# Attention with a routed mixture of experts on one core: the prefix product of the routing two steps later, the last four tiles of expert outputs transposed one step earlier

## The chip, the cores and the metric

The kernel runs on one core of a Trainium2 chip. The metric is the device time of one execution in microseconds (us). The core has five engines that run their own instruction lists and meet at semaphores: TensorE (PE in the rows; PEld is its loading of weights, which runs beside its products), VectorE (DVE), ScalarE (ACT), GpSimd (POOL), and SyncE (SP), which here only issues DMAs. Each engine takes its list in order, so an instruction that waits holds up all that stand behind it.

## The reference

2048 rows of 128 numbers are normalised, and two branches are added to the input: attention of all rows over all rows, and a feed-forward part in which each row goes to the two best of eight experts.

```python
xn = layernorm(x)                                   # x: (1, 2048, 128)
q, k, v = split(xn @ w_qkv.T, 3)                    # one head of width 128
attn = softmax(q @ k.T * scale) @ v @ w_proj.T + b_proj
t = xn @ W_in + b_in
probs = softmax(t @ W_gate + b_gate)                # 8 experts
topv, topi = top_k(probs, 2); topv /= sum(topv)
mid = relu(t @ W1[e] + b1[e]); eout = mid @ W2[e] + b2[e]   # 128 -> 512 -> 128
moe = sum over the two chosen e of topv * eout
out = x + attn + (moe @ W_out + b_out)
```

## The kernel before

**Attention.** The queries go in eight groups g = 0 to 7 of 256. Each group takes eight steps k = 0 to 7, and a step is two key tiles of 128: `scores(i)` is six PE products (L794 to L796, operands split in a high and a low part) into one of three PSUM banks, ACT takes the exponential into `pf` (L455), and `values(i - 2)` multiplies it with the rows, two steps late. In groups 0 to 3 a values product is L919; from group 4 on (the split form) ACT also writes `ph` (L454), DVE makes `pl = pf - ph` (`low(i)`, L613), and values are L928, L929 and L932. Before a group's scores can begin, its row maxima must be known: four `pair` products of 1024 scores (PE L855), each reduced by DVE (`pair_max`, L603), then `row_max` (L608) and `max_row` (PE L863). From group 1 on a pair may start only when DVE has reduced the one before, since all use the same two banks. `PAIR_STEP` lists in which steps of group g the pairs of group g + 1 stand: 4, 5, 5 and 6 in group 0; 1, 2, 4 and 5 after that. Of two pairs in a step, the first stands ahead of the values product, the second behind it. `out_rows` (PE L949), `scale_out` (DVE L619, L622), `project` (PE L963) and `add_out` (DVE L630) finish a group; ACT's `copy_u` (L462) comes before them.

**Routing.** DVE finds both experts of every row (`route_first`, `route_second`, L645 to L657). PE's `prefix` (L970, L971) multiplies the counts with a triangle and with ones; DVE's `route_slots` (L663 to L679) makes of it the slot of every row. POOL then scatters the rows to their slots in DRAM (L353, 32 indirect DMAs) and copies weights of experts (L343).

**Experts.** After group 3, PE works through 39 tiles of 128 slots (L1027 transposes a tile `xg`, L1039 is layer 1, L1053 layer 2). SP stores each result (L262).

**Combining.** When the last store has landed, POOL fetches for each row tile j = 0 to 15 the two expert outputs (`z`, two indirect DMAs, L380) and multiplies one by its gate (`weigh`, L375). DVE adds the other (`combine(j)`, L758). Four tiles make a block b. PE transposes a block (`moe_transpose`, L1083, into bank `MX`), ACT copies it (`cT_copy`, L515), PE multiplies it by W_out (`moe_project`, L1091, into the bank behind), and DVE adds it to the output (`moe_add`, L765). This runs beside groups 4 to 7; their 32 steps are numbered s = 0 to 31. `weighed_at(s)` says which tiles DVE combines in step s, and `BLOCK_AT` in which step PE transposes which block. Within a step DVE's order is: the pairs' maxima, `low`, `q_low`, `scale_out` or `add_out`, the combinations, `moe_add`.

**The order** is written out by hand in every engine's list. `z` lies in the memory of the expert table (`wtab`), so the rows call it `wtab`.

The whole end of the run before the change, on PE:

```python
            values(LAST - 2)
            values(LAST - 1)
            moe_transpose(NR - 1, FIRST_PAIR[NG])
            for r in range(ROUNDS[NG - 1]):
                out_rows(NG - 1, r)
                if r == 0:
                    moe_project(NR - 1)
                project(NG - 1, r)
```

Of the kernel before, what the change touches and what calls it, by code (L numbers as in the profile page):

```python
# [12 lines left out]
def attention_moe_kernel(nc, x, w_qkv, w_proj, b_proj, w_in, b_in, w_gate, b_gate,  # L13
# [6 lines left out]
    NT = S // P  # L20
# [3 lines left out]
    NR = S // BK  # L24
# [19 lines left out]
    NG = len(GROUPS)  # L44
# [6 lines left out]
    FIRST_PAIR = [sum(PAIRS[:g]) for g in range(NG + 1)]  # L51
# [17 lines left out]
    def pairs_at(g, k):  # L69
        return [m for m, at in enumerate(PAIR_STEP[g]) if at == k]  # L70
# [1 line left out]


    def weighed_at(s):
        return [j for j in range(NT) if 5 + (13 * (j + 1)) // 8 == s]

    BLOCK_AT = {14: 0, 22: 1, 26: 2}

    ctx = ExitStack()
    with ctx:  # L80
# [200 lines left out]
        def _(pool):  # L281
# [69 lines left out]
            for n in range(TOPK * NT):  # L351
                j, c = n // TOPK, n % TOPK
# [20 lines left out]
            def weigh(j):  # L373
                pool.wait_ge(s_z[j], 32)
                pool.tensor_scalar(z[:, j, 0, :], z[:, j, 0, :], gate1[:, j:j + 1], None, ALU.mult).then_inc(Z["z_weighed"], 1)  # L375

            pool.wait_ge(Z["gates_ready"], 1)
            for j in range(NT):
                for c in range(TOPK):
                    pool.indirect_dma_start(out=z[:, j, c, :], out_offset=None, in_=slots_out,  # L380
                                            in_offset=bass.IndirectOffsetOnAxis(ap=slots[:, c, j:j + 1], axis=0)
                                            ).then_inc(s_z[j], 16)
                if j >= 2:
                    weigh(j - 2)
            weigh(NT - 2)
            weigh(NT - 1)

        @block.scalar
        def _(act):
# [75 lines left out]
            def beside(g, k):  # L465
                if k == 0 and g + 1 < NG:
                    q_high(g + 1)
                if k == 1 and g not in (0, PRE):
                    copy_u(g - 1)
# [41 lines left out]
            def cT_copy(b):  # L511
                act.wait_ge(Z["cT_done"], b + 1)
                if b >= 1:
                    act.wait_ge(Z["wo_done"], b)
                act.activation(cT[:, :], ps[:, MX, :], ACT.Copy).then_inc(Z["cT_copied"], 1)  # L515

            for g in range(PRE, NG):
                for k in range(STEPS[g]):
                    s = FIRST[g] + k - BASE_B
# [3 lines left out]
                    beside(g, k)  # L523
                    if s in BLOCK_AT:
                        cT_copy(BLOCK_AT[s])
            copy_u(NG - 1)
            cT_copy(NR - 1)

        @block.vector
        def _(dve):  # L530
# [177 lines left out]
            for g in range(PRE):  # L708
                for k in range(STEPS[g]):
                    for m in pairs_at(g, k):  # L710
                        pair_max(g + 1, m)
                    if k == PAIR_STEP[g][-1]:
                        row_max(g + 1)
                    if FIRST[g] + k >= PLAIN:
                        low(FIRST[g] + k)
                    if k == 0:
                        q_low(g + 1)
                    if g > 0:
                        tail(g, k)
                    if g == 0 and k == 1:  # L720
                        route_slots()
                    if g == 1 and k == 0:
                        route_experts()
                    if g == 1 and k == 1:
                        route_gates()
# [35 lines left out]
            def moe_add(b):  # L761
                at = x_sb[:, TB * b:TB * (b + 1), :]
                dve.wait_ge(Z["wo_done"], b + 1)
                dve.wait_ge(Z["x_added"], min(NG - 1, sum(q < BK * (b + 1) for q, _ in GROUPS)))
                dve.tensor_tensor(at, ps[:, MX + 1, :].rearrange("p (j e) -> p j e", e=D), at, ALU.add).then_inc(Z["moe_added"], 1)  # L765

            for g in range(PRE, NG):
                for k in range(STEPS[g]):
                    i = FIRST[g] + k
                    s = i - BASE_B  # L770
                    for m in pairs_at(g, k):
                        pair_max(g + 1, m)
                    if g + 1 < NG and k == PAIR_STEP[g][-1]:
                        row_max(g + 1)
                    low(i)
                    if k == 0 and g + 1 < NG:
                        q_low(g + 1)
                    if g > PRE:
                        tail(g, k)
                    for j in weighed_at(s):  # L780
                        combine(j)
                    if s - 1 in BLOCK_AT:
                        moe_add(BLOCK_AT[s - 1])
            for r in range(ROUNDS[NG - 1]):
                scale_out(NG - 1, r)
            moe_add(NR - 1)
            dve.wait_ge(Z["moe_added"], NR)
            add_out(NG - 1).then_inc(Z["x_added"], 1)

# [1 line left out]
        def _(pe):  # L791
# [191 lines left out]
            def step_pair(g, k, m):  # L983

                if m == 0:
                    pe.wait_ge(Z["q_hi_ready"], g + 2)
                blocks = sum(at < FIRST[g] + k - BASE_B for at in BLOCK_AT)
                if g >= PRE and blocks > 0:
# [17 lines left out]
            for g in range(PRE):  # L1006
                for k in range(STEPS[g]):
                    i = FIRST[g] + k
                    before(g, k)
                    scores(i)  # L1010
                    if g == 0 and k == 1:
                        prefix()
                    beside(g, k)
                    if i >= 2:
                        values(i - 2)
                    for m in pairs_at(g, k)[1:]:
                        step_pair(g, k, m)
                    if g > 0:
                        after(g, k)
# [59 lines left out]
            def moe_transpose(b, pairs):  # L1079
                pe.wait_ge(Z["c_ready"], TB * (b + 1))  # L1080
                pe.wait_ge(Z["max_read"], pairs)
                for j in range(TB):
                    last = pe.transpose(ps[:, MX, P * j:P * (j + 1)], z[:, TB * b + j, 0, :], ident[:, 0:P])  # L1083
                last.then_inc(Z["cT_done"], 1)

            def moe_project(b):
                pe.wait_ge(Z["cT_copied"], b + 1)
                if b >= 1:
                    pe.wait_ge(Z["moe_added"], b)
                for j in range(TB):  # L1090
                    last = pe.matmul(ps[:, MX + 1, P * j:P * (j + 1)], cT[:, P * j:P * (j + 1)], wo_sb[:, :], start=True, stop=True)  # L1091
                last.then_inc(Z["wo_done"], 1)

            for g in range(PRE, NG):
                for k in range(STEPS[g]):
                    i = FIRST[g] + k
                    s = i - BASE_B
# [6 lines left out]
                    beside(g, k)  # L1104
                    if s in BLOCK_AT:
                        moe_transpose(BLOCK_AT[s], FIRST_PAIR[g + 1] + sum(at <= k for at in PAIR_STEP[g]))
# [7 lines left out]
                        after(g, k)  # L1114
            values(LAST - 2)
            values(LAST - 1)
            moe_transpose(NR - 1, FIRST_PAIR[NG])
            for r in range(ROUNDS[NG - 1]):
                out_rows(NG - 1, r)
                if r == 0:  # L1120
                    moe_project(NR - 1)
                project(NG - 1, r)


# [25 lines left out]
```

## Time and profile before

| | |
|---|---|
| median of 3 runs | 242.93 us (242.74 to 244.58) |
| the profiled execution's own time | 244.16 us |
| its span in the profile | 242.4 us |
| PE busy | 227.4 us, 94% |
| DVE, ACT, POOL busy | 137.0 us (56%), 111.6 us (46%), 141.1 us (58%) |
| mean granted clock of TensorE | 0.993 of full speed |

The span is what the profile shows from the first to the last instruction; the own time holds 1.76 us more. Stretches of the span, from the timeline: the normalisation and routing until about 35 us, groups 0 to 3 until about 96, the experts until about 173, groups 4 to 7 with the combination until the end.

### The profile page before, as it was taken

To read this page: it belongs to the slowest core of one execution; us is meant where nothing else is said; L and a number is where in the kernel's file an instruction comes from. 1 tells how busy PE (TensorE), PEld (TensorE's weight loads), DVE (VectorE), ACT (ScalarE), POOL (GpSimd) and SP (SyncE) were. 2 spreads that over 40 slices of the span, in tenths; PEclk is the share of its full clock that TensorE was granted. 3 is DMA by queue.
4 is the path that set the end of the run, shared out by engine and by line. 5 is a ranking of instruction groups with operands and counts; after the bars stand their busy time and mean duration, and the time that the engine had idled before them with its cause. 6 is when DMAs were issued, how large, how long until landed. Compare 5 with 4: busy or idle time off the path is not lost.

```text
span 242.4 us, 4828 instructions
## 1 busy us (share of the span) xinstructions
PE 227.4 (94%) x1724; PEld 215.3 (89%) x1724; DVE 137.0 (56%) x330; ACT 111.6 (46%) x265; POOL 141.1 (58%) x163
## 2 busy tenths in 40 slices
PE   7789498899999999899999999999899989999994
PEld 7688396799999999899999999999899889899993
DVE  5978666275243441444454444544586786895652
ACT  2572322332433423444544445444657537656561
POOL 3159007889888810155666556663078888888700
PEclk9999979999999999999999999999999999999999
DMA  6799901110111120012222222221111111313111
GB/s 189 291 324 337 317 11 46 45 43 33 47 43 43 35 82 26 11 55 67 69 74 70 72 74 65 75 68 47 32 44 36 41 37 58 73 35 83 39 43 43
DMA packets 23047, 19.54 MB, mean 81 GB/s; under 512 B 3280, under 2 KB 19696, under 8 KB 22768
## 3 DMA queue, kind: packets, MB, share of 16 engines
q1 hardware_dynamic: 20000, 14.71, 20.0%
q0 software_dynamic: 2048, 4.20, 6.3%
q10 hardware_dynamic: 976, 0.33, 0.5%
q8 instruction: 14, 0.23, 0.4%
q14 instruction: 9, 0.07, 0.1%
HBM read 10.97 MB, written 8.26 MB: 79 GB/s over the span
## 4 chain that ended last, share of the span: by engine, by line
PE 77%; DVE 7%; POOL 6%; issue 3%; DMA 3%; ACT 3%; ACTq 1%; POOLq 0%; DVEq 0%
PE ps L1053 14%; PE ps L1039 14%; PE ps L919 11%; PE ps L855 5%; PE ps L794 5%; PE ps L796 5%; PE ps L795 5%; POOL wtab L380 5%; DVE part_max L603 3%; DMA w_raw<-in_L_attn_w_proj_dram 2%; PE ps L932 2%; PE ps L928 2%; PE ps L929 2%; PE ps L1027 2%; PE ps L1091 1%
## 5 line engine op out<-in xcount | busy, mean ns | idle before, releaser
L343 POOL COPY wst<-wtab 128x1156 f32 x39 | 45.0, 1153 | 41.1 <-DVE y_sb L740 41.1
L455 ACT ACTIVATE pf<-ps 128x512 f32<-128x512 f32 x64 | 38.1, 595 | 38.3 <-PE ps L796 38.1
L603 DVE TENSOR_REDUCE part_max<-ps 128x1 f32<-128x1024 f32 x32 | 38.9, 1223 | 15.9 <-PE ps L855 15.7
L380 POOL DMA_INDIRECT wtab<-slots_out,slots x32 | 33.8, 1056 | 16.1 <-DMA slots_out<-y_sb 8.4
L353 POOL DMA_INDIRECT slots_in<-hl,slots x32 | 31.5, 983 | 18.7 <-DVE slots L679 11.8
L794 PE MATMUL ps<-q_hi,xnT_hi 128*128 128x256 f32 x128 | 41.7, 326 | 0.5 <-ACT q_hi L440 0.5
L732 DVE TENSOR_SCALAR mid<-ps,wst 128x128 f32<-128x128 f32 x78 | 23.7, 346 | 32.5 <-PE ps L1039 32.5
L1053 PE MATMUL ps<-wst,mid 128*128 128x128 f32 x312 | 41.3, 275 | 0.7 <-DVE x_sb L630 0.7
L1039 PE MATMUL ps<-xgT,wst 128*128 128x128 f32 x312 | 41.3, 275 | 0.0
L1053 PEld LDWEIGHTS ps<-wst,mid 128*128 128x128 f32 x312 | 38.0, 192 | 0.8 <-ACT mid L495 0.8
L1039 PEld LDWEIGHTS ps<-xgT,wst 128*128 128x128 f32 x312 | 38.0, 192 | 0.1
L796 PE MATMUL ps<-q_lo,xnT_hi 128*128 128x256 f32 x128 | 36.4, 284 | 0.0
L795 PE MATMUL ps<-q_hi,xnT_lo 128*128 128x256 f32 x128 | 36.4, 284 | 0.0
L919 PE MATMUL ps<-pf,xn 128*128 128x256 f32 x128 | 33.7, 387 | 0.0
L454 ACT ACTIVATE ph<-ps 128x512 fp32r<-128x512 f32 x32 | 19.1, 598 | 24.5 <-PE ps L796 24.2
L613 DVE TENSOR_TENSOR pl<-pf,ph 128x512 fp32r<-128x512 f32 x32 | 23.0, 718 | 11.8 <-ACT pf L455 11.8
L495 ACT ACTIVATE mid<-ps,wst 128x128 f32<-128x128 f32 x78 | 24.4, 364 | 7.5 <-PE ps L1039 7.5
L919 PEld LDWEIGHTS ps<-pf,xn 128*128 128x128 f32 x128 | 23.7, 195 | 3.2
L794 PEld LDWEIGHTS ps<-q_hi,xnT_hi 128*128 128x128 f32 x128 | 24.6, 192 | 1.3 <-ACT q_hi L440 0.7
L488 ACT ACTIVATE xgT<-ps 128x128 f32<-128x128 f32 x39 | 10.9, 278 | 31.8 <-PE ps L1027 31.8
L795 PEld LDWEIGHTS ps<-q_hi,xnT_lo 128*128 128x128 f32 x128 | 24.6, 192 | 0.6
L796 PEld LDWEIGHTS ps<-q_lo,xnT_hi 128*128 128x128 f32 x128 | 24.6, 192 | 0.0
(145 smaller groups left out, 339.2 us busy)
## 6 DMA issues: line engine op xcount, KB each, us to landing
wtab<-in_L_ffn_W_dram SPq DMA_DIRECT2D x16, 256.0 KB, 6.0
xg<-slots_in SPq DMA_DIRECT2D x39, 64.0 KB, 2.0
slots_out<-y_sb SPq DMA_DIRECT2D x39, 64.0 KB, 1.5
slots_in<-wst SPq DMA_DIRECT2D x2, 1024.0 KB, 4.9
x_sb<-in_L_attn_x_dram SPq DMA_DIRECT2D x4, 256.0 KB, 4.7
out_dram<-x_sb SPq DMA_DIRECT2D x3, 256.0 KB, 2.4
wtab<-in_L_ffn_b_dram SPq DMA_DIRECT2D x1, 512.0 KB, 7.4
slots_in<-hl,slots POOLq DMA_INDIRECT x32
```

Of the source, the lines that this page charges most:

```text
L343: pool.tensor_copy(wst[:, t % 4, :], wtab[:, bass.ds(experts[t], 1), :].rearrange("p a n -> p (a n)")).then_inc(Z["staged"], 1)
L353: pool.indirect_dma_start(out=slots_in, out_offset=bass.IndirectOffsetOnAxis(ap=slots[:, c, j:j + 1], axis=0), in_=hl[:, j, 0:D], in_offse ...
L380: pool.indirect_dma_start(out=z[:, j, c, :], out_offset=None, in_=slots_out, in_offset=bass.IndirectOffsetOnAxis(ap=slots[:, c, j:j + 1], ...
L455: act.activation(pf[:, i % 3, :], ps[:, st_bank(i), :], ACT.Exp).then_inc(Z["pf_done"], 1)
L495: last = act.activation(mid[:, t % 2, c, :], ps[:, 2 * (t % 2), SL * c:SL * (c + 1)], ACT.Relu, bias=wst[:, t % 4, 2 * DM + D + c:2 * DM + ...
L603: dve.tensor_reduce(part_max[:, g % 2, m // 2, m % 2:m % 2 + 1], ps[:, b:b + 2, :], AX.XY, ALU.max).then_inc(Z["max_read"], 1)
L794: pe.matmul(dst, lh, rh, start=start, stop=False)
L795: pe.matmul(dst, ll, rh, start=False, stop=False)
L796: return pe.matmul(dst, lh, rl, start=False, stop=stop)
L919: last = pe.matmul(dst, xn[:, c, :], pf[:, i % 3, cols(g, h)], start=(first and h == 0), stop=(final and h == CH[g] - 1))
L1039: last = pe.matmul(ps[:, 2 * (t % 2) + h, SL * (c % 2):SL * (c % 2 + 1)], wst[:, t % 4, P * c:P * (c + 1)], xgT[:, t % 2, :], start=True, ...
L1053: last = pe.matmul(ps[:, y_bank(t), 0:D], mid[:, t % 2, c, :], wst[:, t % 4, DM + D * c:DM + D * (c + 1)], start=(c == 0), stop=(c == HC - 1))
```

## The change

It has four parts. (1) `prefix` on PE and `route_slots` on DVE move from step 1 to step 3 of group 0. (2) POOL weighs tile j behind the fetches of tile j + 1, not of j + 2. (3) DVE combines every tile one step earlier. (4) Block 3 is transposed in step 31, ahead of three values products, not behind them; `moe_project(3)` stands right behind the last values product, ahead of `out_rows`; ACT copies the block ahead of `copy_u`, and DVE adds it ahead of `scale_out`.

```diff
     def weighed_at(s):
-        return [j for j in range(NT) if 5 + (13 * (j + 1)) // 8 == s]
-    BLOCK_AT = {14: 0, 22: 1, 26: 2}
+        return [j for j in range(NT) if 4 + (13 * (j + 1)) // 8 == s]
+    BLOCK_AT = {14: 0, 22: 1, 26: 2, 31: 3}
...
-                if j >= 2:
-                    weigh(j - 2)
-            weigh(NT - 2)
+                if j >= 1:
+                    weigh(j - 1)
             weigh(NT - 1)
...
             copy_u(NG - 1)
-            cT_copy(NR - 1)
...
-                    if g == 0 and k == 1:
+                    if g == 0 and k == 3:
                         route_slots()
...
+            moe_add(NR - 1)
             for r in range(ROUNDS[NG - 1]):
                 scale_out(NG - 1, r)
-            moe_add(NR - 1)
             dve.wait_ge(Z["moe_added"], NR)
...
-                    if g == 0 and k == 1:
+                    if g == 0 and k == 3:
                         prefix()
...
             values(LAST - 1)
-            moe_transpose(NR - 1, FIRST_PAIR[NG])
+            moe_project(NR - 1)
             for r in range(ROUNDS[NG - 1]):
                 out_rows(NG - 1, r)
-                if r == 0:
-                    moe_project(NR - 1)
                 project(NG - 1, r)
```

The new file is shorter, so lines behind the first edits are numbered two or more lower. On PE, from the second score product of step 1 of group 0 on, before:

```order
L794 MATMUL ps<-q_hi,xnT_hi 128x256
L795 MATMUL ps<-q_hi,xnT_lo 128x256
L796 MATMUL ps<-q_lo,xnT_hi 128x256
L970 MATMUL ps<-both,tri 128x128
L971 MATMUL ps<-both,ones 128x128
L794 MATMUL ps<-q_hi,xnT_hi 128x256
...
L919 MATMUL ps<-pf,xn 128x256 x2
```

and now, from the last values product ahead of it on (step 2, then step 3):

```order
L917 MATMUL ps<-pf,xn 128x256 x2
L792 MATMUL ps<-q_hi,xnT_hi 128x256
L793 MATMUL ps<-q_hi,xnT_lo 128x256
L794 MATMUL ps<-q_lo,xnT_hi 128x256
L792 MATMUL ps<-q_hi,xnT_hi 128x256
L793 MATMUL ps<-q_hi,xnT_lo 128x256
L794 MATMUL ps<-q_lo,xnT_hi 128x256
L968 MATMUL ps<-both,tri 128x128
L969 MATMUL ps<-both,ones 128x128
L917 MATMUL ps<-pf,xn 128x256 x2
```

Two steps of scores (twelve products) and one values product now stand ahead of `prefix`. DVE's order is the same there, since it has nothing to do in steps 1 to 3 of group 0.

On DVE, steps 8 to 11, before (L758 is a combination, L603 a maximum, L613 `low`, L619 and L622 `scale_out`):

```order
L597 TENSOR_TENSOR q_lo<-ps,q_hi 128x256
L758 SCALAR_TENSOR_TENSOR wtab<-wtab,gate 128x128
L603 TENSOR_REDUCE part_max<-ps 128x1
L613 TENSOR_TENSOR pl<-pf,ph 128x512
L758 SCALAR_TENSOR_TENSOR wtab<-wtab,gate 128x128
L603 TENSOR_REDUCE part_max<-ps 128x1
L613 TENSOR_TENSOR pl<-pf,ph 128x512
L619 RECIPROCAL rinv<-ps 128x2
L622 TENSOR_TENSOR o_sb<-ps,rinv 128x256
```

and now:

```order
L595 TENSOR_TENSOR q_lo<-ps,q_hi 128x256
L756 SCALAR_TENSOR_TENSOR wtab<-wtab,gate 128x128
L601 TENSOR_REDUCE part_max<-ps 128x1
L611 TENSOR_TENSOR pl<-pf,ph 128x512
L601 TENSOR_REDUCE part_max<-ps 128x1
L611 TENSOR_TENSOR pl<-pf,ph 128x512
L617 RECIPROCAL rinv<-ps 128x2
L620 TENSOR_TENSOR o_sb<-ps,rinv 128x256
L756 SCALAR_TENSOR_TENSOR wtab<-wtab,gate 128x128
```

The combination behind `q_lo` was that of tile 1 and is now that of tile 2; the one between the two maxima is gone, and tile 3's comes behind `scale_out`.

On PE, the end of the list from step 31's last score product on, before:

```order
L796 MATMUL ps<-q_lo,xnT_hi 128x256
L928 MATMUL ps<-ph,xn_hi 128x256
...
L932 MATMUL ps<-pl,xn_hi 128x256 x2
L1083 MATMUL ps<-ident,wtab 128x128 x4
L949 MATMUL ps<-wvT,ut 128x130 x2
L1091 MATMUL ps<-wo_sb,cT 128x128 x4
L963 MATMUL ps<-wpT,o_sb 128x128 x2
```

and now:

```order
L794 MATMUL ps<-q_lo,xnT_hi 128x256
L1081 MATMUL ps<-ident,wtab 128x128 x4
L926 MATMUL ps<-ph,xn_hi 128x256
...
L930 MATMUL ps<-pl,xn_hi 128x256 x2
L1089 MATMUL ps<-wo_sb,cT 128x128 x4
L947 MATMUL ps<-wvT,ut 128x130 x2
L961 MATMUL ps<-wpT,o_sb 128x128 x2
```

The four transposes now stand ahead of the three values products of steps 29 to 31, and the projection of the block ahead of `out_rows`.

## Rows read from the trace of the kernel before

**Rows 1.** The page, part 4: share of engines in the chain that ended last.

```profile
PE 77%; DVE 7%; POOL 6%; issue 3%; DMA 3%; ACT 3%; ACTq 1%; POOLq 0%; DVEq 0%
```

**Rows 2.** Timeline of PE, group 0: start us, us, what, [idle before, releaser].

```profile
27.18 0.28 PE L796 MATMUL ps<-q_lo,xnT_hi 128*128 128x256 f32 x1
30.30 0.49 PE L970 MATMUL ps<-both,tri 128*128 128x128 f32 x2 [2.83 <-DVE both L657]
...
36.31 0.62 PE L855 MATMUL ps<-xnT_hi,q_hi 128*128 128x512 f32 x2
...
38.35 0.63 PE L855 MATMUL ps<-xnT_hi,q_hi 128*128 128x512 f32 x2
...
44.57 0.43 PE L863 MATMUL ps<-ident,neg_max 128*128 128x128 f32 x2 [0.64 <-DVE neg_max L608]
```

**Rows 3.** Stretches: length, busy PE, PEld, DVE, ACT, POOL, granted clock, DMA.

```profile
31.30:35.30 4.00, 4.00 (x17) 3.59 (x16) 3.27 (x12) 1.00 (x2) 0.00 (x0) 0.57 0.00 1
...
39.30:45.00 5.70, 4.00 (x21) 2.78 (x20) 3.54 (x4) 0.60 (x1) 4.72 (x7) 1.00 0.15 50
```

**Rows 4.** Timeline of DVE, end of the routing and the first maximum for group 1.

```profile
34.73 0.18 DVE L679 CAST slots<-slot_f 128x32 int32<-128x32 f32 x1
36.98 1.23 DVE L603 TENSOR_REDUCE part_max<-ps 128x1 f32<-128x1024 f32 x1 [2.06 <-PE ps L855]
```

**Rows 5.** Timelines of SP and PE where the experts begin.

```profile
87.25 3.67 SPq L258 DMA_DIRECT2D xg<-slots_in  x8
...
94.27 0.27 PE L1027 MATMUL ps<-ident,xg 128*128 128x128 f32 x1
```

**Rows 6.** POOL's fetches (L380) with min/median/max, then two of its multiplications.

```profile
L380 POOL DMA_INDIRECT wtab<-slots_out,slots x32: 944/1001/1465, 175.7 to 226.9; - x32
...
DMA to landing us min/median/max: 2.5/2.7/3.7
...
187.70 1.05 POOL L375 TENSOR_SCALAR wtab<-wtab,gate 128x128 f32<-128x128 f32 x1
...
230.14 0.61 POOL L375 TENSOR_SCALAR wtab<-wtab,gate 128x128 f32<-128x128 f32 x1 [0.88 <-DMA wtab<-slots_out,slots]
```

**Rows 7.** Timelines of DVE and of PE's weight loads, steps 8 to 11.

```profile
188.87 0.38 DVE L758 SCALAR_TENSOR_TENSOR wtab<-wtab,gate 128x128 f32<-128x128 f32 x1 [0.25 <-POOL wtab L375]
...
191.94 0.39 DVE L758 SCALAR_TENSOR_TENSOR wtab<-wtab,gate 128x128 f32<-128x128 f32 x1 [0.96 <-POOL wtab L375]
...
190.43 0.30 PEld L855 LDWEIGHTS ps<-xnT_hi,q_hi 128*128 128x128 f32 x2 [0.54 <-DVE part_max L603]
...
194.66 0.52 PEld L963 LDWEIGHTS ps<-wpT,o_sb 128*128 128x128 f32 x4 [1.09 <-DVE o_sb L622]
```

**Rows 8.** Timeline of weight loads, step 17.

```profile
208.44 0.30 PEld L855 LDWEIGHTS ps<-xnT_hi,q_hi 128*128 128x128 f32 x2 [0.38 <-issue]
```

**Rows 9.** Timeline from step 31 to the end, by start.

```profile
233.73 0.69 DVE L613 TENSOR_TENSOR pl<-pf,ph 128x512 fp32r<-128x512 f32 x1 [0.49 <-ACT pf L455]
233.74 0.19 PEld L928 LDWEIGHTS ps<-ph,xn_hi 128*128 128x128 f32 x1
...
235.92 0.30 PEld L932 LDWEIGHTS ps<-pl,xn_hi 128*128 128x128 f32 x2 [0.19 <-DVE pl L613]
236.18 0.45 PEld L1083 LDWEIGHTS ps<-ident,wtab 128*128 128x128 f32 x4
...
236.47 0.60 ACT L462 ACTIVATE ut<-ps 128x256 f32<-128x256 f32 x1 [1.32 <-PE ps L932]
...
237.87 0.17 DVE L619 RECIPROCAL rinv<-ps 128x2 f32<-128x2 f32 x1 [1.74 <-PE ps L949]
...
238.56 0.70 PE L963 MATMUL ps<-wpT,o_sb 128*128 128x128 f32 x4
...
238.76 0.69 DVE L765 TENSOR_TENSOR x_sb<-ps,x_sb 128x512 f32<-128x512 f32 x1 [0.26 <-PE ps L1091]
...
239.48 0.42 DVE L630 TENSOR_TENSOR x_sb<-ps,x_sb 128x256 f32<-128x256 f32 x1
```

## The prediction

> **What bounds the kernel now.** I read the chain that ended last first: 77% of it is PE [rows 1], so time is won only where PE waits or runs slowly, and lost wherever a new wait enters its list. Next, PE's timeline in group 0: it begins the last score product of step 1 at 27.18 us, is free at about 27.3, and then stands until 30.30 in front of `prefix`, since DVE has not finished `both`; later `max_row` waits for the maxima (idle 0.64) [rows 2]. The stretches show what that first stand costs beside itself: from 31.3 to 35.3 the granted clock is 0.57 on average, so PE is mostly at 1.2 GHz instead of 2.4; from 39.3 to 45.0 PE is busy 4.00 of 5.70 us in short waits, and the clock stays at 1.00 [rows 3]. The two levels are 0.5 and 1, so four microseconds at 0.57 give up 4 x 0.43 = 1.7 us of PE's work. Third, the stretch of the combination: the weight loads wait 0.54 and 1.09 us in steps 10 and 11 [rows 7] and 0.38 in step 17 [rows 8]. Fourth, the end [rows 9].
>
> **Part 1, prefix two steps later.** Nothing is added. Twelve score products and one values product are now issued in the stand. One step of scores, values and a pair takes 2.04 us (36.31 to 38.35); the pair's rows read 0.62, of which some 0.15 lies under the next product (an estimate), so scores and values are 1.4 to 1.6, and I take 1.58. The first step filled is 1.58, the second scores about 0.8, together 2.4 of the 3.0 us. PE reaches `prefix` at 29.7 and waits 0.6 more. `both` comes when it did, so `prefix` still starts at 30.3, DVE's `route_slots` still ends at 34.73 + 0.18 = 34.91 [rows 4], and POOL's scatters move by nothing.
>
> PE itself is then far ahead. Without the slow clock, the first pair of group 1 comes behind `prefix` (0.46) and one step (1.58): 32.3 where it was 36.31, four microseconds sooner. But its maximum is DVE's, and DVE is in `route_slots` until 34.91. It started that maximum at 36.98 [rows 4]; now it starts at about 34.95. From there the chain is pair, maximum, pair, maximum, each pair waiting for the maximum before it, until `max_row`, and PE's idle in front of `max_row` shows that DVE was the later one there already [rows 2]. The chain keeps its length of 44.57 - 36.98 = 7.6 us. So `max_row` moves from 44.57 to 42.54: **2.03 us earlier**, and the other two of the four microseconds go into a new wait of PE, ahead of the second pair, from 34.5 to 36.2. The gain is bounded by DVE from above (no more than 36.98 - 34.91 = 2.07) and, if nothing else turns up, by 1.8 from below for jitter in hand-overs.
>
> Is it kept? Up to the experts PE waits for nothing but its own ACT and DVE work, all of it shifted with it. The experts' input doesn't move: SP begins the loads at 87.25, and PE takes the first tile at 94.27 with no idle before it; 2 us earlier it still comes 5 us behind the load [rows 5]. The experts are PE's work and the fetches start behind their last store, so they shift too.
>
> **Parts 2 and 3, weighing and combining earlier.** The number of fetches and multiplications stays. In POOL's list one more multiplication stands ahead of each fetch, so fetches come 0.8 us later (0.61 and a hand-over of 0.17), and tile j is weighed 0.8 us behind the time at which tile j - 1 was. Does a multiplication now wait for its fetch? Two fetches of 1.0 with hand-overs of 0.3, the fetch itself and a multiplication lie between: 4.1 us from issue against 2.7 to land, at most 3.7 [rows 6]. No.
>
> DVE combines tile 2 in step 8, where it did tile 1 at 188.87. Tile 1's product was ready at 187.70 + 1.05 = 188.75, so tile 2's is now ready at 189.5 [rows 6, 7]. DVE waits for it some 0.9 us ahead of the first maximum, which delays this maximum by 0.7; PE's second pair waits 1.3 instead of 0.54. But the wait of 0.96 at 191.94 and its 0.35 of work, between the first maximum and `scale_out`, are gone. The sum from old start to `scale_out`: + 0.7 - 0.96 - 0.35 and + 0.3 for the pair's product, which was hidden behind that wait and no longer is. So PE's projection at 194.66 comes **0.3 us earlier**. If POOL's operations are as short as their minima (0.61 not 1.05, 0.94 not 1.3), tile 2 is ready at about 188.0, no wait is left, and it is 1.2; if they are longer than now, it is a loss of some 0.3. I take 0.3, since these are the same addresses in the same order. In step 16 the combination ahead of the first maximum disappears (it moves to 15), so most of the 0.38 in step 17 goes [rows 8]: **0.3**. Other steps: a combination of 0.35 fits in DVE's idle times.
>
> **Part 4, the end.** Transposes in step 31 need all 16 tiles combined. Tile 15 is combined in step 30, behind `low(30)`. That starts at 233.73, exactly when PE has issued the scores of step 31 and is free at 233.74 [rows 9]. With 0.69 for `low` and 0.35 for the combination (0.08 overlap) tile 15 is ready at 234.69; POOL's product is not late, 230.14 + 0.61 + 0.8 = 231.6 [rows 6]. So PE gets **a new wait of 1.0 us**, and behind it, in order, stand three values products that it could have done. Then 0.45 for the transposes, which before ran while ACT copied `ut` and cost nothing. The last values product had 0.19 of waiting for `pl`, and with the hand-over 0.25 is absorbed. Net: the last values product ends 1.0 + 0.45 - 0.25 = 1.2 later, and `copy_u` starts at 237.7 instead of 236.47. `moe_project` needs eight weight loads, 2 x 0.45 = 0.9, from 237.35 on; `ut` comes at 238.26, so it is hidden. DVE now adds the block before the reciprocal: it is busy until 239.25 where the reciprocal could start at 237.87 + 1.2 = 239.07, **+ 0.1 to 0.2**. In return the last addition, which waited behind `moe_add` until 239.48 though the projection was out at 238.56 + 0.70 = 239.26, doesn't wait any more: **- 0.2**. The last part: **+ 1.1**. The last output DMA follows the last addition as before.
>
> **The sum.** - 2.0 - 0.3 - 0.3 + 1.1 = - 1.5. The profiled execution becomes 244.16 - 1.5 = 242.66; it lay 1.23 above the median of the runs, so against that median: 242.93 - 1.5 = **241.4 us**. A measurement of this kernel can tell about 1% (2.4 us) from no change, so this counts as no change.
>
> **Rivals.** (a) *The clock falls again, and it gets slower.* PE now has 0.6, 1.7 and three times about 0.7 us of waiting from 29.7 to 42.5. Against: 5.70 us with 30% idle left the clock at 1.00 [rows 3], and a wait of 1.09 in step 11 did too. For: 1.7 is longer than the waits in these rows that left the clock alone, and it comes soon after another. It would cost what it cost before, 1.7 us, up to 2.0 at four microseconds at half speed, since pair products lie on the chain and a step with its pair then takes longer than a maximum: 241.4 + 1.9 = 243.3. It decides at whether the wait ahead of the second pair is followed by rows with products twice as far apart. The Trainium skill, "TensorE: Matmul & The Clock Gate", section "A second HAM failure mode: psum-queue depth-cycling", says that short idles between groups of matmuls, caused by cycling through PSUM banks, can by themselves make the clock swing between its levels. That is this rival, and [rows 3] speak against it. Chance 0.12.
>
> (b) *The whole front gain arrives.* If the second pair didn't have to wait for DVE, the stand and the slow clock would give 4.1: 239.3. Only a different order on DVE would do that. Chance 0.03.
>
> (c) *POOL is faster than its rows*, and steps 8 to 11 give 1.2 and more, both waits of PE going away: 1.6 - 0.3 = 1.3 more than forecast at most, 240.1 to 240.7. For: the gap between POOL's shortest and longest operations. Chance 0.15.
>
> (d) *The transposes stop PE longer*, because tile 15 is late: from fetches that land late and hold up POOL. Each of 15 would have to lose 0.2 us to use up the 2.7 between 231.6 and 234.3. Or DVE waits 0.5 longer in step 8. That takes the middle's gain: 242.0 to 242.9. Chance 0.1.
>
> The forecast with its own bounds (front 1.8 to 2.1, middle 0.3 to 0.9, end 0.9 to 1.3) is 240.8 to 242.2, chance 0.6. The range takes in (c) and most of (a): 240.0 to 243.3. Faster by over 1% (under 240.5) is (b), most of (c) and a tail of the forecast's: 0.17. Slower by over 1% (over 245.4) needs (a) twice over: 0.04.
>
> **What would show it.** In group 0 the scores L792 to L794 run on to 29.7; `prefix` (L968) starts at 30.3 with an idle of about 0.6; the slots' cast (L677) stays at 34.7; the first maximum (L601) follows it at once, and the second pair (L853) waits some 1.7. `max_row` (L861) is at 42.5. The granted clock is 1.00 throughout. In step 8 a combination (L756) waits for POOL. In step 31 the transposes (L1081) wait 1.0 for the combination, and the time from the last scores to the end is 1.1 longer than before. I am wrong if the clock falls, if slots come at another time, or if PE doesn't wait in step 31.

## The result and the profile after

The changed kernel takes 242.22 us (median of 20 runs, 242.08 to 242.59), the kernel before, measured beside it, 244.28 us (20 runs, 242.53 to 246.04). The ratio is 0.9934, 95% interval 0.9915 to 0.9954: a gain of 0.7%. A single profiled execution of each was read: that of the changed kernel took 242.35 us with a span of 240.6, where that of before took 244.16 with 242.4, so it is 1.8 us shorter. I had forecast 1.5 less, and 241.4 us.

More telling than the medians is how the runs lie. The changed kernel's 20 lie within 0.5 us. Those of before fall in groups: 7 at 242.5 to 242.9, 10 at 244.1 to 244.6, 3 at 245.4 to 246.0. Where those come from is the first question of the experiments, since against the lowest group the change gains 0.5 us only.

The timeline of PE of the changed kernel in group 0 (columns as in [rows 2], which these lines answer to):

```profile
29.66 0.28 PE L794 MATMUL ps<-q_lo,xnT_hi 128*128 128x256 f32 x1
30.46 0.49 PE L968 MATMUL ps<-both,tri 128*128 128x128 f32 x2 [0.52 <-DVE both L655]
...
32.58 0.63 PE L853 MATMUL ps<-xnT_hi,q_hi 128*128 128x512 f32 x2
...
36.26 0.73 PE L853 MATMUL ps<-xnT_hi,q_hi 128*128 128x512 f32 x2 [1.47 <-DVE part_max L601]
...
38.30 0.73 PE L853 MATMUL ps<-xnT_hi,q_hi 128*128 128x512 f32 x2 [0.45 <-DVE part_max L601]
...
40.35 0.73 PE L853 MATMUL ps<-xnT_hi,q_hi 128*128 128x512 f32 x2 [0.60 <-DVE part_max L601]
...
42.59 0.43 PE L861 MATMUL ps<-ident,neg_max 128*128 128x128 f32 x2 [0.65 <-DVE neg_max L606]
```

The stand in front of `prefix` has shrunk from 2.83 to 0.52 us. The first pair of group 1 starts at 32.58, 3.7 us earlier, but the second waits 1.47 for DVE, and `max_row` is at 42.59 instead of 44.57: 1.98 earlier. DVE's timeline says why (it answers to [rows 4]):

```profile
34.89 0.18 DVE L677 CAST slots<-slot_f 128x32 int32<-128x32 f32 x1
34.98 1.22 DVE L601 TENSOR_REDUCE part_max<-ps 128x1 f32<-128x1024 f32 x1
```

The first maximum now follows the cast at once, without the 2.06 us of idle. The stretches of the same execution, beside [rows 3]:

```profile
31.30:35.30 4.00, 3.49 (x22) 3.00 (x20) 3.66 (x13) 1.07 (x2) 0.00 (x0) 1.00 0.01 4
35.30:43.00 7.70, 5.04 (x24) 3.67 (x25) 4.73 (x5) 0.72 (x2) 5.65 (x7) 1.00 0.14 45
```

The granted clock (the number behind POOL's busy time) is 1.00 where it was 0.57, and stays there although PE is busy only 5.04 of 7.70 us in the second stretch. The mean over the whole execution is 0.998 and not 1.00 because the clock falls behind 239 us, where PE has no work left.

The combination, in the timelines of POOL and DVE and of PE's weight loads, which answer to [rows 6 to 8]:

```profile
173.99 1.47 POOL L380 DMA_INDIRECT wtab<-slots_out,slots  x1 [8.37 <-DMA slots_out<-y_sb]
...
186.40 0.78 POOL L375 TENSOR_SCALAR wtab<-wtab,gate 128x128 f32<-128x128 f32 x1
...
187.28 0.39 DVE L756 SCALAR_TENSOR_TENSOR wtab<-wtab,gate 128x128 f32<-128x128 f32 x1 [0.25 <-POOL wtab L375]
...
188.85 0.30 PEld L853 LDWEIGHTS ps<-xnT_hi,q_hi 128*128 128x128 f32 x2 [0.68 <-DVE part_max L601]
...
192.05 0.52 PEld L961 LDWEIGHTS ps<-wpT,o_sb 128*128 128x128 f32 x4
...
205.63 0.30 PEld L853 LDWEIGHTS ps<-xnT_hi,q_hi 128*128 128x128 f32 x2 [0.17 <-issue]
```

Counted from the first fetch (175.70 before, 173.99 now), the projection of step 11 comes at 18.06 instead of 18.96 us and has no wait any more, and the pair of step 17 at 31.64 instead of 32.74.

And the end, by start, which answers to [rows 9]:

```profile
230.18 0.19 PEld L792 LDWEIGHTS ps<-q_hi,xnT_hi 128*128 128x128 f32 x1
...
231.51 0.34 DVE L756 SCALAR_TENSOR_TENSOR wtab<-wtab,gate 128x128 f32<-128x128 f32 x1
...
231.91 0.42 PEld L1081 LDWEIGHTS ps<-ident,wtab 128*128 128x128 f32 x4 [0.93 <-DVE wtab L756]
...
234.75 0.60 ACT L461 ACTIVATE ut<-ps 128x256 f32<-128x256 f32 x1 [1.55 <-PE ps L930]
...
235.64 0.69 DVE L763 TENSOR_TENSOR x_sb<-ps,x_sb 128x512 f32<-128x512 f32 x1 [2.61 <-PE ps L1089]
236.25 0.16 DVE L617 RECIPROCAL rinv<-ps 128x2 f32<-128x2 f32 x1
...
237.72 0.42 DVE L628 TENSOR_TENSOR x_sb<-ps,x_sb 128x256 f32<-128x256 f32 x1 [0.86 <-PE ps L961]
```

PE waits 0.93 us in front of the four transposes, for the combination of tile 15. From the first scores of step 31 to the last addition it is 7.54 us. Before, those scores' first weight load stood at

```profile
233.02 0.19 PEld L794 LDWEIGHTS ps<-q_hi,xnT_hi 128*128 128x128 f32 x1
```

and the last addition at 239.48 [rows 9]: 6.46. The end costs 1.08.

The whole, by stage: - 1.98 until `max_row`, + 0.27 from there to the first fetch (it took 131.13 us before and takes 131.40 now), - 1.13 from the first fetch to the scores of step 31 (57.32 and 56.19), + 1.08 to the last addition. The sum is - 1.76.

### The profile page after: what moved, and what is told of

Same layout as the page of the kernel before. It is cut to its first block, busy times and chain, and to the rows that moved or that the text cites. A ratio compares the mean times of both kernels' runs of the same rounds, so it can differ in the third digit from the quotient of the medians.

```text
span 240.6 us, 4828 instructions
## 1 busy us (share of the span) xinstructions
PE 226.1 (94%) x1724; PEld 214.0 (89%) x1724; DVE 136.6 (57%) x330; ACT 111.7 (46%) x265; POOL 140.9 (59%) x163
## 4 chain that ended last, share of the span: by engine, by line
PE 78%; DVE 8%; DMA 4%; POOL 3%; issue 2%; ACT 1%; ACTq 1%; POOLq 0%; DVEq 0%
PE ps L1051 15%; PE ps L1037 15%; PE ps L917 10%; PE ps L853 6%; PE ps L792 5%; PE ps L793 5%; PE ps L794 5%; DVE part_max L601 3%; PE ps L926 2%; POOL wtab L380 2%; PE ps L930 2%; PE ps L927 2%; DMA w_raw<-in_L_attn_w_proj_dram 2%; PE ps L1025 2%; PE ps L800 2%
## 5 line engine op out<-in xcount | busy, mean ns | idle before, releaser
L380 POOL DMA_INDIRECT wtab<-slots_out,slots x32 | 34.4, 1074 | 15.9 <-DMA slots_out<-y_sb 8.4
L353 POOL DMA_INDIRECT slots_in<-hl,slots x32 | 31.5, 985 | 18.7 <-DVE slots L677 11.7
L792 PE MATMUL ps<-q_hi,xnT_hi 128*128 128x256 f32 x128 | 41.2, 322 | 0.5 <-ACT q_hi L439 0.5
L917 PE MATMUL ps<-pf,xn 128*128 128x256 f32 x128 | 32.7, 379 | 0.0
L917 PEld LDWEIGHTS ps<-pf,xn 128*128 128x128 f32 x128 | 23.0, 189 | 3.1
L853 PE MATMUL ps<-xnT_hi,q_hi 128*128 128x512 f32 x64 | 21.2, 416 | 4.3 <-DVE part_max L601 3.8
```

The lines of the kernel that those rows point to most:

```text
L353: pool.indirect_dma_start(out=slots_in, out_offset=bass.IndirectOffsetOnAxis(ap=slots[:, c, j:j + 1], axis=0), in_=hl[:, j, 0:D], in_offse ...
L792: pe.matmul(dst, lh, rh, start=start, stop=False)
L853: last = pe.matmul(ps[:, pair_bank(g, m) + b, :], q_hi[:, g % 2, P * t:P * (t + 1)], xnT_hi[:, at:at + BK], start=True, stop=True)
L917: last = pe.matmul(dst, xn[:, c, :], pf[:, i % 3, cols(g, h)], start=(first and h == 0), stop=(final and h == CH[g] - 1))
```

## The experiments

All times are medians; the last column is the kernel before, run beside each set.

| kernel | us | range, runs | before |
|---|---|---|---|
| part 1 alone | 242.50 | 242.18 to 242.84, 12 | 244.29, 29 runs |
| parts 1 to 3, old end | 241.23 | 241.18 to 241.36, 6 | the same |
| before, PE kept busy in the stand | 242.67 | 242.55 to 243.03, 12 | the same |
| parts 2 and 3 alone | 243.27 | 241.51 to 244.41, 12 | the same |
| changed, transposes two products later | 241.64 | 241.59 to 241.70, 4 | 244.33, 11 runs |
| changed, first pair ahead of `prefix` | 240.63 | 240.47 to 240.72, 4 | the same |
| parts 1 to 3, first pair ahead | 239.57 | 239.47 to 240.51, 6 | the same |
| parts 1 to 3, experts in step 3 | 241.43 | 241.19 to 241.79, 4 | the same |
| parts 1 and 2 | 241.04 | 240.94 to 241.08, 4 | 244.21, 15 runs |
| parts 1 and 3 | 243.33 | 243.03 to 245.21, 10 | the same |
| parts 1 to 3, experts in step 2 | 241.04 | 240.83 to 241.30, 4 | the same |
| parts 1 to 3, first pair ahead, experts in step 2 | 239.65 | 239.38 to 240.23, 5 | the same |

### The clock: is it the stand that makes the groups?

The kernel before, with one line added:

```diff
                     if g == 0 and k == 1:
+                        keep_warm(12, 4)
                         prefix()
```

> The kernel before with twelve products of ones into an unused PSUM bank ahead of prefix, in the stand, so that PE is busy there; nothing is moved. Theory: the clock falls because PE stands, and this fall, which comes in some executions only, makes the two groups of times of before. With the products the clock stays at 1.00 from 31 to 35, the first pair of group 1 starts at 34.7 instead of 36.3, max_row at 43.0, and all runs lie near 242.6. Rival: the fall has another cause than PE's own idleness, or the groups have: then times stay at 242.7 and 244.4 in turn.

It takes 242.67 us, with all twelve runs within 242.55 to 243.03. The stretches of its trace:

```profile
27.30:30.30 3.00, 2.94 (x27) 2.75 (x25) 2.69 (x12) 0.70 (x2) 0.00 (x0) 1.00 1.14 305
31.30:35.30 4.00, 4.00 (x28) 3.71 (x27) 3.36 (x12) 1.60 (x4) 0.00 (x0) 1.00 0.03 6
```

and its timeline of PE:

```profile
34.80 0.62 PE L855 MATMUL ps<-xnT_hi,q_hi 128*128 128x512 f32 x2
...
43.12 0.43 PE L863 MATMUL ps<-ident,neg_max 128*128 128x128 f32 x2 [0.65 <-DVE neg_max L608]
```

Twelve useless products, which delay `prefix` by no more than 0.09 us (it starts at 30.39), keep the clock at 2.4 GHz behind the stand, bring `max_row` 1.45 us forward and the median 1.6 us down to the lowest group of before. Of the 29 runs of the kernel before beside it, 9 lie at 242.6 to 242.9 with a mean granted clock of 0.998 to 1.00, 14 at 244.1 to 244.5 with 0.991 to 0.993, and 6 at 245.3 to 246.2 with 0.986. So the fall of the clock comes from PE's own standing, it comes in about two runs of three, and it makes the groups. The highest group was in no profile. Its mean clock says that it lost about twice as much clock as the middle one (0.014 of the run instead of 0.007), but not where.

### Part 1 alone

```diff
-                    if g == 0 and k == 1:
+                    if g == 0 and k == 3:
```

The same edit stands in both places, on PE and on DVE.

> The kernel before with part 1 alone: prefix and route_slots in step 3. Theory: PE's scores fill the stand, the slots are ready when they were, and the first maximum of group 1 follows them at once. max_row moves from 44.57 us to about 42.6, the granted clock stays at 1.00 between 31 and 35, the fetches of the combination begin 1.7 to 2.0 earlier, and steps 8 to 11 and the end keep their waits, so the run ends 1.7 to 2.0 earlier than the profiled one before (about 242.5) and its runs lie close together. Rival: the 20 runs of before lie in groups near 242.7 and 244.4, and the difference has another source than the stand; then the runs of this kernel are spread as widely as those of before.

It takes 242.50 us, with all runs within 0.7 us, as the theory had it. PE in its timeline:

```profile
30.24 0.49 PE L970 MATMUL ps<-both,tri 128*128 128x128 f32 x2 [0.54 <-DVE both L657]
...
42.38 0.43 PE L863 MATMUL ps<-ident,neg_max 128*128 128x128 f32 x2 [0.65 <-DVE neg_max L608]
```

But it is only 0.17 us below the kernel with the useless products, with ranges that overlap. The two together split part 1's gain: 1.6 us is the clock that doesn't fall, and of the earlier products themselves 0.2 is left. In the two profiled executions, which lie 0.42 apart (242.25 and 242.67), `max_row` is 0.74 earlier than in the kernel kept busy, 0.15 of it since `prefix` was at 30.24 here and at 30.39 there; 0.3 is lost again on the way to the first fetch (131.41 us against 131.08), which is the next question.

### Where the 0.27 goes

In the changed kernel's timelines of POOL, of DVE and of weight loads, group 1:

```profile
46.22 0.99 POOL L353 DMA_INDIRECT slots_in<-hl,slots  x1 [0.16 <-issue]
...
46.59 0.79 DVE L680 TENSOR_TENSOR cmp<-tile_no,tiles_c 128x320 f32<-128x320 f32 x1
...
48.03 1.22 DVE L601 TENSOR_REDUCE part_max<-ps 128x1 f32<-128x1024 f32 x1
...
49.30 0.30 PEld L853 LDWEIGHTS ps<-xnT_hi,q_hi 128*128 128x128 f32 x2 [0.23 <-DVE part_max L601]
```

In the kernel before the same comparison took 0.48:

```profile
48.58 0.48 DVE L682 TENSOR_TENSOR cmp<-tile_no,tiles_c 128x320 f32<-128x320 f32 x1
```

and no pair waited there. The comparison is the first of three instructions of `route_experts`, which stand ahead of a maximum. Two kernels move them, in parts 1 to 3 with the old end:

```diff
-                    if g == 1 and k == 0:
+                    if g == 1 and k == 3:
                         route_experts()
```

> Parts 1 to 3 with the end of the kernel before, and route_experts in step 3 of group 1 instead of step 0. Theory: 0.27 of part 1's 2.0 is lost in group 1, since an instruction of route_experts on DVE takes 0.79 instead of 0.48 and the first maximum of the group stands behind it, so PE's second pair waits 0.23. Out of the way, PE doesn't wait there: 240.95, 0.25 under the 241.2 of the same kernel without this edit. Rival: the wait at the second pair has another source, and the time stays at 241.2.

It takes 241.43 us against 241.23, so there is no gain. The wait of 0.23 is gone, but now the three stand right ahead of the third maximum, and PE's weight loads show

```profile
55.70 0.30 PEld L854 LDWEIGHTS ps<-xnT_hi,q_hi 128*128 128x128 f32 x2 [0.29 <-DVE part_max L602]
```

My own edit had moved the wait to another pair. With `k == 2`:

> Parts 1 to 3 with the end of the kernel before, and route_experts in step 2 of group 1, behind scale_out, where DVE stands idle for 1.39 us. In step 3 it was right ahead of the third maximum and moved PE's wait there (0.29 in place of 0.23). Theory: now neither wait is left: 240.95 against 241.2. Rival: it stays at 241.2, because the operations that take longer collide wherever they stand.

It takes 241.04 us, and no weight load waits between 45 and 60 us. The medians lie 0.19 apart with ranges that overlap, which is no proof by itself; but from `max_row` (42.67) to the first fetch (173.79) it takes 131.12 us, as in the kernel before, where the same kernel without the edit takes 131.41.

What slows the comparison was not tried, but the traces of all fourteen kernels agree on when it happens. Where it starts 0.36 to 0.63 us behind the start of one of POOL's scatters (L353, as in the lines above: 46.22 and 46.59), it ends 0.16 to 0.18 behind the end of that scatter, and takes 0.53 to 0.80 us for it; that is so in eight kernels. In the other six it starts at another time, and takes 0.48, once 0.53. In the kernel before it starts 0.88 behind one (47.70). POOL's scatters hang on the slots, which part 1 leaves where they were, while the comparison comes 2 us earlier with PE, and so falls on another moment of them. That this is the cause is likely by these rows, but no edit tested it.

### Parts 2 and 3

Both alone, on the kernel before:

> The kernel before with parts 2 and 3 alone: weighing behind the next tile's fetches, combining one step earlier. Theory: it saves what the changed kernel saved between the first fetch and the last scores, 1.1 us by its profile (0.3 to 0.6 was my first estimate), so 1.1 less than before in the same clock state; the projection of step 11 waits for less than 0.3 us where it waited 1.09. Rival: that saving hung on how far PE and POOL were shifted against each other by part 1, and alone it gives 0.5 or less.

It takes 243.27 us. Nine of twelve runs lie at 243.1 to 243.6, 1.1 us below the middle group of before (244.3) and at its clock (0.993); two lie at 244.4, at the clock of the highest group (0.986); and one, at 241.51 with a clock of 1.00, is 1.0 below the fastest run of before. The gain doesn't hang on part 1. Then each without the other, both with part 1 and the old end. Weighing earlier, combining where it was:

```diff
-                if j >= 2:
-                    weigh(j - 2)
-            weigh(NT - 2)
+                if j >= 1:
+                    weigh(j - 1)
             weigh(NT - 1)
```

> Parts 1 and 2 with the end of the kernel before: POOL weighs a tile earlier, DVE combines where it did. Theory: PE's waits of steps 10 and 11 hang on how late DVE gets tile 2 weighed, so POOL's earlier weighing alone takes away DVE's wait in step 9 and most of the gain of 1.1 to 1.3 arrives: 241.2 to 241.6, as with both parts. Rival: the gain is in taking the combination out from between the two maxima, which this kernel leaves there; then it is at 242.0 or more (242.5 is the kernel with part 1 alone).

It takes 241.04 us, 0.2 below the kernel with both parts, with ranges that don't meet. So all of the gain is POOL's earlier weighing, and part 3 beside it costs 0.2. The other one:

```diff
-        return [j for j in range(NT) if 5 + (13 * (j + 1)) // 8 == s]
+        return [j for j in range(NT) if 4 + (13 * (j + 1)) // 8 == s]
```

> Parts 1 and 3 with the end of the kernel before: DVE combines a step earlier, POOL weighs where it did. Theory: tile 2 is weighed at about 189.9 us of this kernel's time while DVE stands for it from step 8 on, ahead of the first maximum; PE loses more than before: 243.5 or more, which is at least 1 more than part 1 alone (242.5). Rival: the earlier place alone gives the gain, 241.2 to 241.6.

It takes 243.33 us, 0.8 above part 1 alone and a little under the 243.5 that the theory asked for. Six of ten runs lie at 243.0 to 243.4 with a mean granted clock of 0.997 to 1.00, four at 244.4 to 245.2 with 0.991 to 0.993. The profiled one is the slowest of all (245.21): 0.9 us of it comes from a later start (`prefix` at 31.10, against 30.24 in part 1 alone), a stage that the edit doesn't touch, and 2.1 lie between the first fetch and the scores of step 31. DVE, the weight loads and the stretches of that execution:

```profile
189.82 0.39 DVE L758 SCALAR_TENSOR_TENSOR wtab<-wtab,gate 128x128 f32<-128x128 f32 x1 [1.76 <-POOL wtab L375]
...
191.40 0.50 PEld L855 LDWEIGHTS ps<-xnT_hi,q_hi 128*128 128x128 f32 x2 [2.59 <-DVE part_max L603]
```

```profile
188.00:191.40 3.40, 1.02 (x9) 0.81 (x8) 1.64 (x4) 1.96 (x4) 2.78 (x4) 0.97 0.13 39
191.40:196.00 4.60, 4.60 (x24) 4.41 (x25) 3.22 (x6) 0.48 (x1) 4.07 (x5) 0.65 0.16 43
```

Tile 2 isn't weighed when DVE asks for it in step 8. PE's next pair waits 2.59 us for the maximum that stands behind that combination, and behind the stand the granted clock is 0.65. It is the same pair of losses as in front of `prefix`, made at another place. By the two groups of runs the stand alone costs about 0.65 us (243.15 in the middle of the six runs, 242.50 with part 1 alone), and the fall of the clock, where it comes, some 1.4 more; both are estimates from few runs.

### Part 4

Parts 1 to 3 with the end of before (the diff is that of the change, without the entry for step 31 and the edits to ACT, DVE and PE at the end):

> Parts 1 to 3 with the end of the kernel before (block 3 transposed behind the last values product). Theory: the change without the part that costs it 1.1 us at the end, so about 241.1 where the change took 242.2; from the last scores to the end it takes 9.4 us as before, where the changed kernel takes 10.4. Rival: the end is bound by the fetches or the output DMA, and undoing part 4 gives nothing: 242.2.

It takes 241.23 us, 0.99 under the changed kernel. From the first scores of step 31 (230.01) to the last addition (236.47) it takes 6.46 us, exactly as in the kernel before. (My expectation's 9.4 and 10.4 are counted to the end of the span, and came out so.) Then the changed kernel with the transposes later:

```diff
             values(LAST - 2)
+            moe_transpose(NR - 1, FIRST_PAIR[NG])
             values(LAST - 1)
             moe_project(NR - 1)
```

Step 31 is taken out of the loop's transposes.

> The changed kernel with the last four transposes two values products later: behind those of steps 29 and 30, ahead of that of step 31. Theory: what part 4 costs is PE's wait for tile 15 and the transposes on its path. Two values products (1.4 us) now cover the wait of 0.9, the transposes of 0.42 stay on the path: 241.3 to 241.5, which is 0.8 under the changed kernel. Rival: the cost lies in moe_project and moe_add standing ahead of out_rows and scale_out; then the time stays at 242.2.

It takes 241.64 us. Its weight loads and the last addition:

```profile
232.38 0.46 PEld L1081 LDWEIGHTS ps<-ident,wtab 128*128 128x128 f32 x4
...
233.76 0.97 PEld L1089 LDWEIGHTS ps<-wo_sb,cT 128*128 128x128 f32 x8 [0.18 <-ACT cT L514]
...
234.65 0.53 PEld L947 LDWEIGHTS ps<-wvT,ut 128*128 128x128 f32 x4
...
237.05 0.42 DVE L628 TENSOR_TENSOR x_sb<-ps,x_sb 128x256 f32<-128x256 f32 x1 [0.86 <-PE ps L961]
```

The wait for tile 15 is gone and brings 0.6 of the 1.0. A new wait of 0.18 for ACT's copy of the block appears in front of `moe_project`, which is why it isn't the 0.8 of the theory.

What remains against the old end is 0.4 (6.85 us from the first scores at 230.20, against 6.46), and it is not the transposes alone. In the kernel with the old end `out_rows` waits for `ut` and for nothing else:

```profile
230.01 0.19 PEld L793 LDWEIGHTS ps<-q_hi,xnT_hi 128*128 128x128 f32 x1
...
234.10 0.52 PEld L948 LDWEIGHTS ps<-wvT,ut 128*128 128x128 f32 x4 [0.49 <-ACT ut L461]
```

Counted from the first scores, `copy_u` starts 0.19 later with the transposes ahead (at 233.83, 3.63 us behind them, against 3.44): that is the part of the transposes. `out_rows` starts 0.36 later (4.45 against 4.09), since it now stands behind the eight loads of `moe_project`, though `ut` is ready 0.2 before that. DVE's reciprocal starts 0.53 later (5.37 against 4.84), since it stands behind `moe_add`. Of this 0.14 comes back, because the last addition no longer waits for `moe_add`. So the rival in the expectation, that `moe_project` and `moe_add` stand in the way, is wrong for most of part 4's cost, but about half of the 0.4 that is left is theirs.

### What bounds group 0 now

If it is DVE's list, a maximum put into DVE's wait for `prefix` must shorten it:

```diff
-    PAIR_STEP = [[4, 5, 5, 6]] + 6 * [[1, 2, 4, 5]] + [[]]
+    PAIR_STEP = [[3, 5, 5, 6]] + 6 * [[1, 2, 4, 5]] + [[]]
...
+                    beside(g, k)
                     if g == 0 and k == 3:
                         prefix()
-                    beside(g, k)
```

> The changed kernel with the first pair of group 1 in step 3, ahead of prefix, its maximum ahead of route_slots. Theory: DVE's list bounds group 0 since part 1. One of the four maxima (2.04 us with its hand-overs) now lies in DVE's wait for prefix, at 30.5, and route_slots comes 0.7 later: max_row at 41.1 to 41.4 instead of 42.6, time 241.0 (1.2 less). Rival: PE or the later stages absorb it, and the time stays within 0.3 of 242.2.

It takes 240.63 us, 1.6 under the changed kernel where the theory had 1.2. DVE's timeline:

```profile
30.47 1.22 DVE L601 TENSOR_REDUCE part_max<-ps 128x1 f32<-128x1024 f32 x1
...
35.29 0.18 DVE L677 CAST slots<-slot_f 128x32 int32<-128x32 f32 x1
```

`route_slots` ends 0.4 later, not the 0.7 of the theory, and `max_row` is at 40.95, 1.64 earlier: that is the 2.04 of one maximum with its hand-overs less 0.4. With the old end:

> Parts 1 to 3 with the end of the kernel before, and the first pair of group 1 ahead of prefix. Theory: both savings add up: 241.2 less 1.2 is 240.0. Rival: the slots come 0.7 later and the experts wait for them; then 240.7 or more.

It takes 239.57 us; neither the experts nor the scatters took it back. Four of the six runs lie at 239.5 to 239.6 with a mean granted clock of 1.00, two at 240.2 and 240.5 with 0.993. The profiled one (240.23) shows in PE's timeline and in its stretches

```profile
36.70 0.73 PE L854 MATMUL ps<-xnT_hi,q_hi 128*128 128x512 f32 x2 [1.19 <-DVE part_max L602]
...
38.74 0.93 PE L854 MATMUL ps<-xnT_hi,q_hi 128*128 128x512 f32 x2 [0.60 <-DVE part_max L602]
```


```profile
36.00:38.00 2.00, 1.30 (x8) 1.16 (x8) 1.18 (x2) 0.00 (x0) 1.30 (x2) 1.00 0.00 0
38.00:42.00 4.00, 3.40 (x12) 2.41 (x11) 2.07 (x3) 0.68 (x2) 3.08 (x4) 0.64 0.14 49
```

a granted clock of 0.64, behind waits of no more than 1.19 us. It costs 0.7. And last, with `route_experts` in step 2 as well:

> Parts 1 to 3, the end of the kernel before, the first pair of group 1 ahead of prefix, and route_experts in step 2 of group 1. Theory: 239.5 less 0.25 is 239.3, and the clock of group 0 may fall in some runs as it did in the profiled one of the kernel without the last edit (240.23 against 239.5). Rival: 239.5 as without it.

It takes 239.65 us. The ratio to before is 0.9820 (0.9794 to 0.9846), 1.8% faster; against the lowest group of before (242.8) it is 1.3%. It is 2.6 us under the changed kernel. By the times the last edit can't be told from nothing here (239.38 to 240.23 against 239.47 to 240.51). By the stages it holds: from `max_row` to the first fetch it takes 131.08 us, where the changed kernel with the first pair ahead took 131.45. The clock fell in one of the five runs (240.23, mean clock 0.993). The kernel still has part 3, which cost 0.2 beside part 2; without it, it was not run.

## Why the prediction was right, and where it was not

**The forecast.** It said 1.5 us less, which is no change by its bound of 1%; the profiled executions differ by 1.8 and the medians by 2.1. The range of 240.0 to 243.3 held 242.22, at the very end of the forecast's own bounds (242.2). That the sum was so close is partly luck, since the middle gained 0.5 more than forecast and group 1 lost 0.27 that was not in the sum. The absolute number was 0.8 too low, and the step behind that is the last one of the sum: I took 1.5 from the median of the runs I was given, 242.93, and called the 1.23 between it and the profiled execution a shift of both kernels. It was the fall of the clock. Two of those three runs lie in the lowest group, where the clock doesn't fall, so most of part 1's gain could not be taken from them. From a run of that group the change takes 0.5.

**Part 1, front.** `prefix` at 30.3 (30.46), idle 0.6 (0.52), the cast where it was (34.89), the first maximum at once, the second pair's wait 1.7 (1.47), `max_row` at 42.54 (42.59): each as forecast, and DVE was the bound, as the pair ahead of `prefix` shows by breaking it. What the forecast did not separate is where the 2.0 comes from: useless products in the stand already bring 1.45 of it, so most of it is the clock, and the useful work moved into the stand is worth little because DVE bounds what follows. "Is it kept?" was answered too lightly: 0.27 went in group 1, where an instruction of DVE's `route_experts` takes longer, most likely because the scatters didn't shift with it. I had looked only at PE's waits, not at how close DVE was to making one.

**Parts 2 and 3, middle.** Forecast 0.6, measured 1.13. The terms: steps 8 to 11 gave 0.90, not 0.3; the stretch up to step 17 gave another 0.20, not 0.3. DVE does wait for tile 2 in step 8, but 0.25 and not 0.9 us, since tile 2 is ready 13.2 us behind the first fetch and not 13.8. That the same addresses in the same order would take the same time was the wrong reason: the eight fetches ahead of that multiplication took 8.38 us together, where they had taken 9.14. I had also left in the hand-over of 0.30 between two fetches, which goes where a multiplication now stands between them. Against that, the first multiplication waits 0.23 for its fetch, where my answer to "does it wait?" was no. This is rival (c), in part. And the mechanism was wrong in one point: I counted a gain to DVE's new order, while the weighing alone gives all of it.

**Part 4, end.** Forecast + 1.1, measured + 1.08, by the steps given: a wait of 1.0 (0.93), `copy_u` 1.2 later (1.12), the reciprocal held up by the block's addition (236.25, right behind 235.64 + 0.69 less the overlap), and the last addition freed from its wait. The kernel with the old end confirms it by 0.99.

**Rival (a), the clock.** By their times it came in none of the 20 runs of the changed kernel (mean granted clocks of 0.996 to 1.00, without relation to the time). My argument against it, that short waits had left the clock alone, was not a safe one: with the first pair moved, waits of 1.19 and 0.60 us were followed by a clock of 0.64 in the profiled run, and three of the fifteen runs of the three kernels with that front show such a loss. The rule of the Trainium skill cited above ("TensorE: Matmul & The Clock Gate", "A second HAM failure mode: psum-queue depth-cycling"), that short idles between groups can make the clock swing, agrees with that kernel and not with the changed one. Why one kernel meets it and the other doesn't stays open.

## What to carry to other kernels

Before a predicted saving is taken from a measured median, ask whether the profiled execution and the median's runs are of the same kind; times in groups some 1.6 us apart, each group with its own mean granted clock, say they are not. TensorE's stand of 2.8 us cost 1.6 us more behind it, and useful products moved into it, or even useless ones, took that part away. Instructions that are moved forward in PE's list cost nothing only if their inputs are ready there: in step 31 the combination of a tile ended almost a microsecond after PE asked for it, and all products behind it paid. And a saving on one engine shifts its instructions against those of an engine that doesn't move, and here one of them then took longer.

## What the runs showed of the hardware

A stand of TensorE of 2.83 us is followed by a granted clock of 0.57 over 4 us in the profiled execution. In 9 of 29 other runs of the same program the mean granted clock (0.998 to 1.00) and the time show no such fall; 1.6 us is its price here. A stand of 2.59 was followed by 0.65, and by the times in 4 of 10 runs. Waits of 1.47, 0.45, 0.60 and 0.65 in a row were not followed by a fall in the changed kernel; waits of 1.19 and 0.60 were in another, in 2 of 6 runs. The same DVE comparison of 128x320 elements takes from 0.48 to 0.80 us; it is longer when it starts 0.36 to 0.63 us behind the start of an indirect DMA of POOL, and then ends 0.16 to 0.18 behind that DMA's end. POOL's 32 indirect DMAs of the combination take 0.94 to 1.47 us each for the same work.
